# First attention layer of a fused hybrid block rebuilt: row maximum from a first score pass, exponent scores produced transposed, one q/k/v projection

## What is computed

```python
# layer 0: shifted-window attention, 12 heads of 8 channels, windows of 8 x 8 = 64 tokens
xn  = group norm of x                      # 32 groups of 3 channels over an image
q, k, v = xn @ qkv_w.T + qb
qn = q / norm(q);  kn = k / norm(k)        # over the 8 channels of a head
attn = einsum('whid,whjd->whij', qn, kn) * exp(min(logit_scale, log 100)) + bias
attn = attn + mask                         # -100 between regions of a shifted window
x = x + proj(softmax(attn) @ v)
# layer 1: banded attention, 6 heads of 16 channels, on layer norm of x
# layer 2: mixture of 4 experts (top 2), hidden size 384, on layer norm of x
```

## Time and profile before

| | us |
|---|---|
| median of three runs (lowest, highest) | 501.06 (499.53, 501.89) |
| the profiled execution, its time | 497.59 |
| its span in the trace | 493.5 |
| PE busy | 433.9 (88%) |
| DVE busy | 362.0 (73%) |
| ACT busy | 335.1 (68%) |
| POOL busy | 131.6 (27%) |

### The profile page before, as it was taken

One profiled execution on the slowest core, in us unless ns is written; L12 is line 12 of the kernel. 1 busy time (PEld: TensorE's weight loads), 2 busy tenths in 40 slices (PEclk: granted clock), 3 DMA queues, 4 the chain that ended last, 5 costly groups with the idle time before them and its releaser, 6 DMA issues.

```text
span 493.5 us, 14736 instructions
## 1 busy us (share of the span) xinstructions
PE 433.9 (88%) x5354; PEld 324.2 (66%) x5354; DVE 362.0 (73%) x1056; ACT 335.1 (68%) x898; POOL 131.6 (27%) x257
## 2 busy tenths in 40 slices
PE   2547999999999996889999999788998999999995
PEld 1114767777776765667777777566885677777773
DVE  4976778787888788457767777647677777777776
ACT  1016787777778785268888888555777777777773
POOL 8302222222121226033433334553912000000000
PEclk9999999999999999589999999997999999999998
DMA  7112000000000000000000000000500232212300
GB/s 174 23 30 71 28 8 0 0 0 1 0 0 0 0 0 2 1 2 3 3 0 0 0 0 0 2 1 1 129 2 17 68 81 80 57 25 80 80 14 18
DMA packets 14326, 12.36 MB, mean 25 GB/s; under 512 B 12803, under 2 KB 13143, under 8 KB 13528
## 3 DMA queue, kind: packets, MB, share of 16 engines
q1 hardware_dynamic: 13128, 11.74, 9.3%
q10 hardware_dynamic: 1072, 0.08, 0.2%
q0 software_dynamic: 96, 0.14, 0.1%
HBM read 10.31 MB, written 1.70 MB: 24 GB/s over the span
## 4 chain that ended last, share of the span: by engine, by line
PE 65%; ACT 10%; DVE 10%; SPq 6%; issue 4%; DMA 2%; POOL 1%; DVEq 0%; ACTq 0%
PE bank L651 8%; PE bank L663 6%; PE score_banks L718 5%; PE score_banks L1283 4%; PE score_banks L1280 4%; PE score_banks L1281 4%; PE bank L684 3%; PE bank L708 3%; PE bank L590 3%; PE score_banks L1269 3%; PE score_banks L625 3%; PE score_banks L1270 3%; ACT probsT L816 3%; PE score_banks L1271 3%; PE score_banks L606 2%
## 5 line engine op out<-in xcount | busy, mean ns | idle before, releaser
L985 POOL TENSOR_TENSOR stack<-qk,ones 128x192 f16<-128x192 f32 x64 | 32.4, 506 | 183.2 <-DVE qk L907 115.4
L1432 DVE TENSOR_TENSOR hidden_lo<-hidden,hidden_hi 128x512 fp32r<-128x512 f32 x96 | 65.6, 685 | 20.1 <-ACT hidden_hi L1336 20.0
L839 DVE TENSOR_REDUCE negmax<-score_banks 128x12 bf16<-128x768 f32 (+1 forms) x64 | 48.2, 754 | 25.7 <-PE score_banks L625 25.7
L651 PEld LDWEIGHTS bank<-vals,probsT 128*64 128x64 f32 (+1 forms) x1536 | 36.9, 127 | 29.0 <-ACT probsT L813 19.1
L651 PE MATMUL bank<-vals,probsT 128*64 128x18 f32 (+1 forms) x1536 | 42.5, 208 | 13.9 <-ACT probsT L816 4.5
L1334 ACT ACTIVATE hidden<-score_banks 128x512 f32<-128x512 f32 x64 | 38.3, 598 | 21.7 <-PE score_banks L1271 17.7
L718 PE MATMUL score_banks<-perm,probs 128*128 128x128 f32 x288 | 43.9, 281 | 0.7 <-ACT probs L786 0.7
L663 PE MATMUL bank<-w_qkv,xnT 128*128 128x192 f32 x128 | 40.2, 398 | 3.9 <-DVE qk L907 3.0
L1280 PE MATMUL score_banks<-hidden_hi,w_hi 128*96 128x512 f32 x96 | 38.6, 402 | 2.2 <-ACT hidden_hi L1336 2.2
L1283 PE MATMUL score_banks<-hidden_lo,w_hi 128*96 128x512 f32 x96 | 38.5, 401 | 1.7 <-DVE hidden_lo L1432 1.7
L813 ACT ACTIVATE probsT<-score_banks 128x384 f32<-128x384 f32 x32 | 15.7, 490 | 34.4 <-PE score_banks L718 34.4
(11 more groups left out here) (195 smaller groups left out, 1105.5 us busy)
## 6 DMA issues: line engine op xcount, KB each, us to landing
xT_all<-gate_scratch SPq DMA_DIRECT2D x8, 768.0 KB, 5.2
x_all<-in_x SPq DMA_DIRECT2D x4, 384.0 KB, 7.3
out<-moe_final SPq DMA_DIRECT2D x8, 192.0 KB, 2.2
w<-in_w SPq DMA_DIRECT2D x1, 582.0 KB
w<-in_w SPq DMA_DIRECT2D x1, 576.0 KB
bias_f<-col_scratch SPq DMA_DIRECT2D x16, 24.0 KB
perm<-in_permutations SPq DMA_DIRECT2D x1, 320.0 KB, 3.2
w_qkv<-in_w_qkv SPq DMA_DIRECT2D x2, 109.1 KB
```

The lines of the kernel that those rows point to most:

```text
L651: last = pe.matmul(o_bank[rows, pair_of[h2] * 2 * vd:(pair_of[h2] + 1) * 2 * vd], probsT[:, h2, rows], buffer_of(k, odd, -1)[:, w, pair_of ...
L839: v.tensor_reduce(negmax[:].rearrange("p (g h) -> p g h", g=2), score_banks[k][:, :, 0:half].rearrange("p g (h j) -> p g h j", j=KEYS), AX ...
L1432: v.tensor_tensor(hidden_lo[m % HBUF][:], hidden[m % 2][:], hidden_hi[m % HBUF][:], ALU.subtract).then_inc(q["hidden_lo"], 1)
```

## The change

Layer 0 gets a function of its own, `window_attention`; `attention` keeps layer 1. In layer 0:

- q, k and v come from one projection of 288 columns into one bank (`pe_project`); that bank is free for the next unit when DVE has scaled q and k and ACT has copied v. ACT's order in a step becomes Exp, squares, four copies of v, Ln, Exp, one copy of the transposed stack.
- The Newton step of the norm moves from DVE to POOL (`pool_root`), and the high part of k moves from ACT to POOL (`pool_stacks`). `stack` has two buffers, and its last 8 columns of a head hold the mask's one-hot code (`slot_tail`), so that the score products carry the mask.
- A first score pass (`pe_scores`, 24 products, without the bias) serves only for the row maximum. DVE writes the negated maximum into a column of q's stack, PE transposes q's stack again (three transposes), DVE copies it (`qmT`).
- A second pass (`pe_logits`, six products with the bias and 24 small ones) gives bias, mask, scores and maximum in transposed form. Exp writes `probsT` directly. The six fp32 transposes of probabilities, their two copies, the two products that add the maximum and the four for bias and mask are gone.
- POOL makes the stack of unit n + 1 in step n, where it made that of unit n + 2; so its last step of layer 0 is 30 and not 29.
- In both layers the residual is added to `x_all` in place and the statistics go straight to `ln_half`; the two copies behind them are gone.
- The set-up has one rounding and one subtraction of the bias, on 64 partitions, where it had two sums, two roundings and two subtractions; only `pe_logits` of unit 0 waits for it. DVE copies `slot_tail` into both stacks before `tables_set`.

```diff
-    def pe_step(pe, b, k, odd):                       # layer 0's part
-        pe_scores(pe, n, b, k, ahead_x)               # holds pe_project_qk between its two halves
-        if k == 0:
-            pe_output_project(pe, n - 1, b - 1)
-        else:
-            pe_output_transpose(pe, n - 1, b)
-        pe_probs_transpose(pe, n - 1, 1 - k)
-        pe_stacks(pe, n)
-        pe_project_v(pe, n + 1, 1 - k, ...)
-        pe_shift(pe, n, k)
-        pe_values(pe, n, b, k, odd)
+    def pe_step(pe, b, k, odd):
+        n = 2 * b + k
+        pe_scores(pe, n, k, 0)
+        if k == 0:
+            pe_output_project(pe, n - 1, b - 1)
+        else:
+            pe_output_transpose(pe, n - 1, b)
+        pe_scores(pe, n, k, 1)
+        pe_project(pe, n, b, k, xnT[:, (1 - odd) * T:(2 - odd) * T])
+        pe_values(pe, n, b, k, odd)
+        pe_maximum(pe, n, k)
+        pe_stacks(pe, n, k)
+        pe_logits(pe, n, k)
...
+    def pe_project(pe, n, b, k, x):
...
+            at_least(pe, q["qk_ready"], n + 2)
+            at_least(pe, q["v_ready"], n + 2)
+            pe.matmul(qkv_bank[:, 0:3 * C], x[:, k * P:(k + 1) * P], w_qkv[:], start=True,
+                      stop=True).then_inc(q["qkv_ready"], 1)
...
+    def act_step(act, b, k, odd):
+        n = 2 * b + k
+        act_exp(act, n)
+        act_squares(act, n)
+        act_values(act, n, k, odd)
+        act_norm_guess(act, n)
+        act_transposed_stacks(act, n, k)
...
+    def dve_step(v, b, k, odd):
+        n = 2 * b + k
+        dve_scale(v, n)
+        if k == 0:
+            dve_residual(v, n - 1, b - 1)
+        else:
+            dve_output(v, n - 1, b)
+        dve_max(v, n, k)
+        dve_sum_squares(v, n)
+        dve_maximum(v, n)
+        dve_divide(v, n, b, k)
+        if k == 0:
+            dve_statistics(v, n, b)
+        else:
+            dve_group_norm(v, n, b, odd)
...
+    def pool_root(pool, n):
...
+            nc.gpsimd.tensor_tensor(newton[:], guess[:], guess[:], ALU.mult).then_inc(q["newton_step"], 1)
+            at_least(pool, q["newton_step"], 3 * n + 7)
+            nc.gpsimd.tensor_tensor(newton[:], newton[:], sumsq[:], ALU.mult).then_inc(q["newton_step"], 1)
+            at_least(pool, q["newton_step"], 3 * n + 8)
+            nc.gpsimd.tensor_tensor(guess_scaled[:], guess[:], s["head_scale"][:], ALU.mult)
+            nc.gpsimd.tensor_scalar(newton[:], newton[:], -0.5, 1.5, ALU.mult, ALU.add).then_inc(q["newton_step"], 1)
+            at_least(pool, q["newton_step"], 3 * n + 9)
+            nc.gpsimd.tensor_tensor(rnorm[:], newton[:], guess_scaled[:], ALU.mult).then_inc(q["rnorm_ready"], 1)
...
-            steps(pool, a0["pool"], N - 4, N - 2)
+            steps(pool, a0["pool"], N - 4, N - 1)
```

More of the change, by code:

```diff
@@ L163, in set_once_pool, with set_values @@
+SET_VALUES = [3 * n for n in VALUE_BUFFERS]
+SET_ONCE = sum(SET_VALUES) + 3
+def set_values(pool, nc, bufs, layer, done):
+    vals, d = bufs["vals"], VALUE_SHAPES[layer][2] - 1
+    start = sum(SET_VALUES[:layer]) + 3 * layer
     for v in vals:
         nc.gpsimd.memset(v[:], 0.0).then_inc(done, 1)
-    nc.gpsimd.memset(bufs["ones"][:], 1.0).then_inc(done, 1)
-    pool.wait_ge(done, start + 2 + len(vals))
+    pool.wait_ge(done, start + len(vals))
     for v in vals:
@@ new lines, in pe_scores @@
+            for g in range(2):
+                pe.matmul(S[:, g, 0:half].rearrange("p (t j) -> p t j", t=TILES3), ident_bf[:],
+                          s["band"][:, k, None, :].to_broadcast([P, TILES3, KEYS]),
+                          start=True, stop=False, skip_group_check=True)
+            for t in range(TILES3):
+                for g in range(2):
+                    rows = slice(slot * g, slot * (g + 1))
+                    for w in range(NQB):
+                        part, k0 = slice(w * QBLOCK, (w + 1) * QBLOCK), k * P + w * QBLOCK
+                        last = pe.matmul(S[part, g, t * KEYS:(t + 1) * KEYS], qT[rows, t, part],
+                                         kT[rows, t, k0:k0 + KEYS], start=False, stop=True, skip_group_check=True)
@@ L659, in pe_project_qk @@
             at = halo + k * P
-            if k == 0 and (first or not on(n)):
+            if k == 0 and not on(n):
                 at_least(pe, q["xnT_ready"], b + 2)
@@ L1120, in _ @@
             setup["weights_ready"](pe)
[L1121 to L1125 removed]
+            steps(pe, a0["pe"], -2, 4)
             middle_steps(pe, a0["pe"])
```

581 lines of the change are left out of this document (337 added, 244 removed).

## The result

The changed kernel took **507.95 us** in the median of five runs (502.85 to 526.09), beside 499.53 (493.43 to 501.89) for the kernel before on the same chip. Forecast were 491 us, a range of 480 to 505 and a faster kernel; all five runs are slower than all of before.

The account below looks back on a forecast made before the run. PE was taken as all but full in regular steps, the norm loop nearly as long, with a stall at layer 0's end. Terms 1.4 + 1.8 - 10.7 - 1.0 - 1.5 = -10.0 us, against 501.06 gave 491 us; range 480 to 505.

Parts of the forecast that it names:

- PE in a regular step: Regular steps of layer 0: PE work falls to about 3.9 us from 4.5, worth nothing beyond what the next loops allow.
- norm loop: Layer 0, from one projection to the next through norm and scaling: 4.92 us against 4.87, +1.4 us over 27 steps.
- rival 4: End of layer 0 gains little, by a falling clock or DVE held elsewhere: 3 and not 10.7 us, 499 us; 8%.
- five cases: Four rivals and the forecast itself, a loop of 4.7 to 5.2 us with 486 to 499 us, 50%.
- rival 2: POOL's root in layer 0 is cheap and the loop falls to a second one at 4.45 us: 478 us; 15%.
- second loop: Layer 0 step through Exp, the copy of transposed columns and 24 score products to the next projection: 4.45 us.
- rival 1: POOL's root, between guess and scaling in layer 0, is the bound: loop of 5.65 us, 511 us, slower; 14%.
- rival 3: Group norm on DVE and POOL's root hinder each other in odd steps: loop grows by 0.2 us, 496 us; 13%.
- The Trainium skill's rule on GpSimd: POOL's root at twice DVE's time, 0.36 us an instruction: loop about 5.3 us, +11 us over the forecast value.
- The end of layer 0: From projection of unit 31 to the first of layer 1: 13.9 us in place of 24.61, so -10.7 us.
- The head: Set-up until the projection of unit 2: 45.2 us against 43.46, so +1.8 us, bounds 0 and +3.
- Layer 1: Two DVE copies fewer in every other step, -1.5 us; its first 3 us no longer at slow clock, -1.0.

Follow-up runs that it names:

- the first profiled run: The changed kernel itself, unaltered, the slowest of its first five runs: 524.0 us span.
- narrow_bias: Kernel before with its four bias and mask products of a step fed by 32 rows in place of 128: 503.6 us.
- fill_f32: Changed kernel with six more fp32 transposes of the identity, read by nobody, in each step of layer 0: 487.2 us.
- head_two: Changed kernel with twelve wide fp16 products, read by nobody, in each of steps 0 to 3 and two in each later step of layer 0: 471.9 us.
- head_one: Changed kernel with twelve wide fp16 products in each of steps 0 to 3 and one in each later step of layer 0: 474.6 us.
- head_none: Changed kernel with twelve wide fp16 products in each of steps 0 to 3 of layer 0 and none later: 487.3 us.
- head_small: Changed kernel with twelve wide fp16 products in each of steps 0 to 3, then sixteen small ones (32 rows, 64 columns) in each later step: 472.7 us.
- head_rows32: Changed kernel with twelve wide fp16 products in each of steps 0 to 3, then four on 32 rows in each later step: 481.9 us.
- again: Changed kernel once more, unaltered, for a second profile: 483.8 us.
- fill_wide: Changed kernel with four more wide fp16 products (128 rows, 256 columns), read by nobody, in each step of layer 0: 476.9 us.
- fill_small: Changed kernel with 24 more small fp16 products (64 columns), read by nobody, in each step of layer 0: 498.3 us.

## Why the prediction was wrong

**The step that failed** is the first of the part on PE in a regular step, "about 3.9 us of PE work in a step instead of 4.5", and with it the sum of the norm loop. The size holds at full clock: 53.02 of 60.00 us busy at 4.36 us a step are 3.85 us. (Its own terms give about 3.7, not 3.9.) But all its durations come from full-clock rows, and it took for granted that the clock stays full with other work. The clock was weighed only in rival 4, for the end, and tied to idle time. In the changed kernel 3.9 us of work become 6.1 whenever the clock is down, PE becomes the bound, and neither loop matters. Of the slices of the earlier trace rows below full it named two; a third, 7 tenths at about 335 us, it passed over. None of the five cases held this one; 1.4 us for the loop was 35.5 in the first profiled run. The sum also had no term for ACT's wait for the weights (1.31 and 3.41 us in two of the three profiles).

**The norm loop** at full clock is 4.36 us and not 4.92. Its own rows, in the run of 483.8 us:

```profile
109.62 0.22 ACT L704 ACTIVATE log_sum<-sumsq 128x24 f32<-128x24 f32 x1
...
110.18 0.22 POOL L828 TENSOR_TENSOR newton<-guess 128x24 f32<-128x24 f32 x1 [0.78 <-ACT guess L706]
...
111.00 0.21 POOL L833 TENSOR_SCALAR newton<-newton 128x24 f32<-128x24 f32 x1
111.29 0.23 POOL L835 TENSOR_TENSOR rnorm<-newton,guess_scaled 128x24 f32<-128x24 f32 x1
111.71 0.36 DVE L728 TENSOR_TENSOR qk<-bank,rnorm 128x192 f32<-128x192 f32 x1 [0.85 <-POOL rnorm L835]
```

From the projection at 107.73: Ln at +1.89 (2.04 forecast), root at +2.45 (2.60), root over at +3.79 (4.40), next projection at +4.40. The root takes 1.34 us, not 1.8: the one with two constants costs 0.21, no more than the others. That is rival 2 in kind, with its second loop (4.45 forecast) as near as the first: in this step the next projection also stands directly behind the 24 score products, the first of which waited for ACT's copy. The loop of rival 1 (5.65) is out, and rival 3 cost nothing: DVE's group norm (L789, 110.39 to 110.87) runs beside the root, which takes 1.34 us in steps with and without it. L789 itself takes 0.48 us there, where L929 took 0.40 in before.

**The Trainium skill's rule on GpSimd** (GPSIMD Engine Reference, section Engine selection) that the prediction weighed gave 0.36 us an instruction; measured are 0.21 to 0.23, against DVE's 0.17 to 0.18. At 24 columns the factor of two does not show; POOL's 0.22, 0.37 and 0.51 us at 24, 96 and 192 columns leave most of the 0.22 to a part that doesn't grow with the width, an estimate from these rows.

**The end of layer 0** was right in kind: 13.9 us forecast (its terms add up to 13.7); 12.7 at full clock, 18.1 at half. **The head**: 45.2 us forecast for unit 2, 45.20 measured in that run. The exact hit is luck: the first projection came 0.4 us later than forecast and the way from it to unit 2 was 0.4 shorter, and in other runs that projection stood at 30.7 in place of 34.2 (with before's code at 29.7 in narrow_bias, 33.3 else), so the start moves by 3.5 us by itself. **Layer 1** and what follows: -2.5 forecast, -0.2 to -2.2 in the three profiled runs of the changed kernel. With fill it was up to +3.8 (fill_f32), so this term is not resolved.

At a clock that holds, the sum is this (head_two against the profiled run of before): head -1.8, 29 steps 131.4 against 141.7, -10.3, end 13.0 against 24.6, -11.6, rest -0.9: -24.5 us. Some 3.5 us of it are the start that moves by itself, so -21; the medians say 25 (0.951). Where the clock holds, change and fill together are worth 4 to 5%; the kernel before with the same fill, whose first steps and end also run partly at half clock, was not measured, so the change's own part may be less. As it stands its median is 1.5% above before's, and the runs lie on both sides of it, as the clock falls early, late or often.

**What is shown and what isn't.** Shown: the same program runs steps of 4.36 or 6.1 us by PE's clock alone; one added product a step holds it in the regular steps (head_one against head_none, four runs each that don't overlap); in the kernel before, narrower products bring dips at the same busy share. So what PE does in a step decides, and busy share alone does not. By what measure is open: head_small and fill_f32 speak against width alone. After the change PE idles more at full clock (12% against 4%) and has lost its 384-column products; each points the same way, and their shares were not separated. Once down, the clock stayed down at 99 to 100% busy: the Trainium skill, TensorE: Matmul & The Clock Gate, section What's actually happening, has activity release the throttle, and busy time as a profile counts it is not that activity here. Open too: how often ACT's wait for the weights is what brings the clock down (a kernel with L1269 a step later was not run), and what made one run of head_rows32 differ.

## What to carry to other kernels

A change that takes work off a nearly full PE can cost the clock at which its times were measured: before trusting a sum of full-clock durations, work it out at half clock too, and ask whether PE would then be the bound. If the spread of the runs grows, look at the duration of one fixed product over time, not at busy shares or the mean clock. Where slack remains, a little idle work for PE, more at the head and one or two wide products a step, may pay many times over: here, besides the twelve products in each of the first four steps, 0.04 us a step for 33 us. And a kernel that starts a layer sooner can arrive at a load before it has landed: look for such waits where the steps got shorter.

## What was not expected of the hardware

- PE was 99% busy for 170 us at 1.2 GHz (168.89 of 170.00 us, 52 to 222 us of the first profiled run) and its clock did not rise. In all seven profiles with twelve products of 256 columns in the first steps the clock was full by 51 us and stayed so for 90 us and more; without them it was full by 50 us as well in some (before, 49.7; the first profiled run, for 3.4 us), but in others only at 57 (again), 105 (fill_wide) or 136 us (fill_small). In head_two the twelve took 2.56 us at 42.80 and 1.48 us at 48.83.
- The granted clock reads full until its first recorded change: in fill_wide's profile 1.00 in the window 80 to 100 us, where L579 takes 1.33 us in place of 0.75.
- Small and fp32 filler went with a full clock in the regular steps as wide fp16 filler did (472.7 and 487.2 us); one run of the 32-row kind took 532 us.
